# A quantised convolution network: VectorE convolves two of eight tiles, ScalarE writes the normalised rows, the down projection moves one slot later

## What is computed

```python
x = x + _L1_ffn_ref(_layernorm(x), w1, conv_w, conv_b, w2)

def act_quant(x):
    scale = 127.0 / clip(max(abs(x), axis=-1), 1e-05)
    return clip(round(x * scale), -128, 127) / scale
h = bit_linear(x, w1)                       # act_quant(x) @ ternary w1, 256 -> 1024
h = depthwise_conv1d(h, conv_w, conv_b)     # 3 taps along the sequence, one set per channel
h = silu(h)
x_add = bit_linear(h, w2)                   # act_quant(h) @ ternary w2, 1024 -> 256
```

## Time and profile before

| | |
|---|---|
| median of 3 runs | 1712.03 us (1707.19 to 1712.98) |
| the profiled execution | 1712.71 us, span 1710.6 us |
| busy, share of the span | PE 86%, PEld 64%, DVE 61%, ACT 44%, POOL 7% |
| this stage | first up projection at 511.98, last residual ends at 674.14 |
| mean granted TensorE clock | 0.941 of full speed |

### The profile page before, as it was taken

How to read it: one execution, slowest core, us unless ns; L and a number is a source line. 1 busy time by engine, 2 the same in 40 slices (tenths; PEclk the granted TensorE clock), 3 DMA queues, 4 the chain that set the end, 5 groups by cost and what they waited for, 6 DMA issues and landing times.

```text
span 1710.6 us, 27127 instructions
## 1 busy us (share of the span) xinstructions
PE 1475.4 (86%) x9940; PEld 1101.9 (64%) x9947; DVE 1035.3 (61%) x2319; ACT 749.7 (44%) x1249; POOL 111.5 (7%) x153
## 2 busy tenths in 40 slices
PE   6999999878879895799889999999988999997356
PEld 4666665557764443477767878787864777786345
DVE  4455564778868764787746161625248988975434
ACT  2211212267763664676732122222224877885122
POOL 1000000000000000111000000000001101000323
PEclk9999999999989997999989999999998999998579
DMA  9451101400000000000029600000100000000176
GB/s 323 160 172 61 61 14 48 165 13 13 13 2 1 0 1 12 12 13 13 2 104 341 187 1 2 1 2 2 32 7 6 2 7 7 2 2 1 48 256 224
DMA packets 59540, 99.82 MB, mean 58 GB/s; under 512 B 10739, under 2 KB 48748, under 8 KB 59246
## 3 DMA queue, kind: packets, MB, share of 16 engines
q1 hardware_dynamic: 57022, 82.57, 14.8%
q10 hardware_dynamic: 512, 11.11, 1.9%
q0 software_dynamic: 1872, 4.27, 0.7%
HBM read 76.23 MB, written 38.35 MB: 67 GB/s over the span
## 4 chain that ended last, share of the span: by engine, by line
PE 49%; issue 23%; DVE 12%; ACT 5%; DVEq 4%; DMA 3%; POOL 1%; SPq 1%; ACTq 1%; POOLq 1%
PE bank L1906 7%; PE bank L1907 7%; PE bank L1611 6%; PE bank L1628 5%; PE bank L1965 3%; PE bank L1712 3%; PE bank L1763 2%; DVE MB L844 2%; DVE plo L862 2%; DMA jx<-copy_routed 2%; PE bank L1683 1%; PE bank L1645 1%; PE bank L1717 1%; PE bank L1716 1%; DVEq L1120 1%
## 5 line engine op out<-in xcount | busy, mean ns | idle before, releaser
L862 DVE TENSOR_TENSOR plo<-e,phi 120x512 f16<-120x512 f32 x256 | 179.9, 708 | 46.6 <-ACT phi L1363 43.3
L1357 ACT ACTIVATE e<-bank 120x512 f32<-120x512 f32 x256 | 150.6, 588 | 39.3 <-PE bank L1717 32.1
L1363 ACT ACTIVATE phi<-e 120x512 f16<-120x512 f32 x256 | 161.5, 631 | 8.8
L844 DVE TENSOR_REDUCE MB<-bank 128x4 bf16<-128x480 f32 x256 | 156.2, 649 | 14.4 <-PE bank L1685 10.5
L1611 PE MATMUL bank<-xT,winT 128*127 128x512 f32 (+1 forms) x256 | 114.8, 594 | 4.7 <-ACTq L1276 4.7
L1628 PE MATMUL bank<-woutT,msk 128*128 128x256 f32 (+1 forms) x512 | 115.2, 379 | 0.0
L1305 ACT ACTIVATE act<-bank,bin 127x512 f32<-127x512 f32 x64 | 43.6, 687 | 151.6 <-DVE dec L732 145.1
L1628 PEld LDWEIGHTS bank<-woutT,msk 128*128 128x128 f32 (+1 forms) x512 | 97.0, 190 | 16.3 <-DVE msk L724 0.3
L1906 PE MATMUL bank<-hah,h1w 128*128 128x512 f32 x256 | 101.3, 396 | 3.3 <-DVE hal L654 3.3
L548 POOL TENSOR_TENSOR veps<-mv,ceps 128x4 f32<-128x4 f32 x32 | 6.4, 201 | 1483.6 <-DVEq L622 1346.9
L1712 PE MATMUL bank<-Q_even,Kpad_even 128*120 128x256 f16 x512 | 100.6, 279 | 2.0 <-ACT e L1357 2.0
(11 more groups left out here) (305 smaller groups left out, 3606.3 us busy)
## 6 DMA issues: line engine op xcount, KB each, us to landing
copy_routed<-zeros SPq DMA_DIRECT2D x1, 17028.0 KB
jw<-copy_experts SPq DMA_DIRECT2D x23, 641.0 KB
seen<-in_h1T SPq DMA_DIRECT2D x8, 512.0 KB, 5.6
seen<-in_h2T SPq DMA_DIRECT2D x8, 512.0 KB, 6.3
h1w<-copy_h1T SPq DMA_DIRECT2D x1, 4096.0 KB, 17.0
h2w<-copy_h2T SPq DMA_DIRECT2D x1, 4096.0 KB, 14.1
ctxp<-in_ctxT SPq DMA_DIRECT2D x13, 240.0 KB, 2.8
jx<-copy_routed SPq DMA_DIRECT2D x23, 132.0 KB
```

Source lines behind the costliest of these rows:

```text
L844: dve.tensor_reduce(MB[:, t, h0 // 8, SK + h0 % 8:SK + h0 % 8 + 4], b[:, 0:4 * SK].rearrange("p (h k) -> p h k", h=4), AX.X, ALU.max).then ...
L862: dve.tensor_tensor(plo[:, g % 3, :], e32[:, g % 3, :], phi[:, g % 3, :], ALU.subtract).then_inc(s.lo, 1)
L1357: act.activation(e32[:, g % 3, :], bank[2 + g % 3][0:SK, :], ACT.Exp).then_inc(s.exp, 1)
L1363: act.activation(phi[:, g % 3, :], e32[:, g % 3, :], ACT.Copy).then_inc(s.phi, 1)
```

## The change

VectorE convolves tiles 0 and 4 of each pair itself (`conv_tile`): a tensor_scalar for the first tap and two scalar_tensor_tensor for the others, written straight into hc; TensorE leaves these tiles out, and the tap matrices for them are not built. `convolved(g)` picks the semaphore of the engine that convolved a tile. silu of such a tile reads and writes hc. `next_rows` goes from VectorE to ScalarE (slot 1), with `shift` for the fourth stage on GpSimd, and `quantise_rows` waits for it. `down` moves from slot 0 to slot 1 on TensorE, `down_residual` from slot 1 to slot 2 on VectorE.

```diff
--- before.py
+++ after.py
@@ -35,6 +35,7 @@
 CELL = D + 8
 JOBS = NT + NE - 1
 NB, NO = 6, 4
+VTILES = (0, 4)
 SEEN = (2 * K2 + 2 * HT) // PAIRS
 W1, W2, B1, B2, KIT = 0, K2 * D, 2 * K2 * D, 2 * K2 * D + K2, 2 * K2 * D + K2 + D
 
@@ -349,8 +350,8 @@
     Ff.xs, Ff.m0, Ff.g1, Ff.low, Ff.lowsum, Ff.long = (
         sem("f_" + n) for n in ("xs", "m0", "g1", "low", "lowsum", "long"))
     Df = Signals()
-    Df.xq, Df.xqt, Df.xqT, Df.sb, Df.sB, Df.up, Df.deq, Df.conv = (
-        sem("d_" + n) for n in ("xq", "xqt", "xqT", "sb", "sB", "up", "deq", "conv"))
+    Df.xq, Df.xqt, Df.xqT, Df.sb, Df.sB, Df.up, Df.deq, Df.conv, Df.vconv = (
+        sem("d_" + n) for n in ("xq", "xqt", "xqT", "sb", "sB", "up", "deq", "conv", "vconv"))
     Df.silu, Df.mag, Df.maxed, Df.mt, Df.dgh, Df.qb, Df.hm, Df.hq, Df.out = (
         sem("d_" + n) for n in ("silu", "mag", "maxed", "mt", "dgh", "qb", "hm", "hq", "out"))
     Hf = Signals()
@@ -374,6 +375,10 @@
             s.oT, s.oTs, s.out, s.half, s.bo = (sem(L.name + "_" + n) for n in ("oT", "oTs", "out", "half", "bo"))
         X[L.name] = s
     X["l3x"] = X["l2x"]
+
+    def convolved(g):
+        n = sum(q % HT in VTILES for q in range(g + 1))
+        return (Df.vconv, n) if g % HT in VTILES else (Df.conv, g + 1 - n)
 
     def next_pair(i):
         return (i + 1) % PAIRS
@@ -568,7 +573,7 @@
                                        ALU.add).then_inc(X["l2x"].bo, 1)
                 if p == 2:
                     pool.wait_ge(xln_ready, 4 * p + i + 1)
-                rstd_of(i + (4 * p + 2), p in (2, 4, 6))
+                rstd_of(i + (4 * p + 2), p in (2, 3, 4, 6))
 
         pool.iota(acc[:, 0, :], pattern=[[PLACES // 128, NE]], base=0, channel_multiplier=0,
                   allow_small_or_imprecise_dtypes=True)
@@ -982,6 +987,7 @@
             def quantise_rows(i):
 
                 dve.drain()
+                dve.wait_ge(xln_ready, 4 * 3 + 1 + i)
                 dve.tensor_reduce(amax[:], xln[:], AX.X, ALU.max, apply_absolute_value=True)
                 dve.drain()
                 quantiser(0)
@@ -1006,7 +1012,7 @@
                     dve.wait_ge(Df.sB, i + 1)
                 dve.wait_ge(Df.up, g + 1)
                 if g >= 3:
-                    dve.wait_ge(Df.conv, g - 2)
+                    dve.wait_ge(*convolved(g - 3))
                 dve.tensor_tensor(hpad[:, g % 3, :, 1:S + 1], bank[g % 2][:, :].rearrange("p (b s) -> p b s", b=2),
                                   sB[:, i % 2, :].rearrange("p (b s) -> p b s", b=2), ALU.mult).then_inc(Df.deq, 1)
 
@@ -1017,6 +1023,16 @@
                     before = mags[:, (g - 1) % 2, :] if t == 1 else mrun[:, i % 2, :]
                     last = dve.tensor_tensor(mrun[:, i % 2, :], mags[:, g % 2, :], before, ALU.max)
                     last.then_inc(Df.maxed, 1 if t > 1 else 2)
+
+            def conv_tile(g):
+                t, y = g % HT, hc[:, g // HT % 2, g % HT, :].rearrange("p (b s) -> p b s", b=2)
+                dve.drain()
+                dve.tensor_scalar(y, hpad[:, g % 3, :, 0:S], cw[:, t, 0:1], None, ALU.mult)
+                for j in (1, 2):
+                    dve.drain()
+                    last = dve.scalar_tensor_tensor(out=y, in0=hpad[:, g % 3, :, j:j + S], scalar=cw[:, t, j:j + 1],
+                                                    in1=y, op0=ALU.mult, op1=ALU.add)
+                last.then_inc(Df.vconv, 1)
 
             def quantise_hidden(i):
                 dve.wait_ge(Df.mt, i + 1)
@@ -1052,13 +1068,6 @@
                 for t in range(TT):
                     dve.bn_aggr(mv[:, t, :], stats[:, t, :])
                 dve.drain().then_inc(ln_var, 1)
-
-            def next_rows(i):
-                dve.wait_ge(ln_rstd, i + (4 * 3 + 2))
-                for t in range(TT):
-                    dve.tensor_scalar(xln[:, t, :], x[:, TT * next_pair(i) + t, :],
-                                      mv[:, t, 0:1], rstd[:, t:t + 1], ALU.subtract, ALU.mult)
-                dve.drain().then_inc(xln_ready, 1)
 
             dve.memset(magic[:, 0:1], MAGIC)
             dve.memset(magic[:, 1:2], -MAGIC)
@@ -1071,16 +1080,16 @@
                 i, t = g // HT, g % HT
                 dve.drain()
                 if g < TILES3:
-                    if i == 0:
+                    if i == 0 and t not in VTILES:
                         tap_weights(t)
                     dequantise(g)
+                if g < TILES3 and t in VTILES:
+                    conv_tile(g)
                 if 2 <= g < TILES3 + 2:
                     largest(g - 2)
                 if t == 0 and i < PAIRS:
                     next_stats(i)
-                if t == 1 and i < PAIRS:
-                    next_rows(i)
-                if t == 1 and i >= 2:
+                if t == 2 and i >= 2:
                     down_residual(i - 2)
                 if t == 2 and i < PAIRS - 1:
                     quantise_rows(i + 1)
@@ -1417,10 +1426,11 @@
 
             def silu(g):
                 i, t = g // HT, g % HT
-                act.wait_ge(Df.conv, g + 1)
+                act.wait_ge(*convolved(g))
                 if i >= 2 and t == 0:
                     act.wait_ge(Df.hm, HT * (i - 1))
-                act.activation(hc[:, i % 2, t, :], bank[2 + g % 2][:, :], ACT.Silu,
+                y = hc[:, i % 2, t, :] if t in VTILES else bank[2 + g % 2][:, :]
+                act.activation(hc[:, i % 2, t, :], y, ACT.Silu,
                                bias=cb[:, t:t + 1]).then_inc(Df.silu, 1)
 
             def magnitude(g):
@@ -1429,6 +1439,14 @@
                     act.wait_ge(Df.maxed, g - 1)
                 act.wait_ge(Df.silu, g + 1)
                 act.activation(mags[:, g % 2, :], hc[:, i % 2, t, :], ACT.Abs).then_inc(Df.mag, 1)
+
+            def next_rows(i):
+                act.wait_ge(Df.xq, i + 1)
+                act.wait_ge(ln_rstd, i + (4 * 3 + 2))
+                for t in range(TT):
+                    last = act.activation(xln[:, t, :], x[:, TT * next_pair(i) + t, :], ACT.Identity,
+                                          bias=nmr[:, t:t + 1], scale=rstd[:, t:t + 1])
+                last.then_inc(xln_ready, 1)
 
             def rounded(g):
                 i, t = g // HT, g % HT
@@ -1446,6 +1464,8 @@
                 if 1 <= g <= TILES3:
                     silu(g - 1)
                     magnitude(g - 1)
+                if t == 1 and i < PAIRS:
+                    next_rows(i)
                 if t == 3 and i < PAIRS - 1:
                     dequant_scales(i + 1)
                 if t == 4 and i < PAIRS - 1:
@@ -1872,9 +1892,9 @@
                 i, t = g // HT, g % HT
                 if g < TILES3:
                     up(g)
-                if 1 <= g <= TILES3:
+                if 1 <= g <= TILES3 and (g - 1) % HT not in VTILES:
                     conv(g - 1)
-                if t == 0 and i >= 2:
+                if t == 1 and i >= 2:
                     down(i - 2)
                 if g == TILES3:
                     pe.wait_ge(xln_ready, 4 * 3 + 5)
```

## The result

The changed kernel takes 1719.98 us (median of 7 runs, 1717.63 to 1726.89) beside 1709.92 for the kernel before in the same session (7 runs, 1705.86 to 1713.53). The ratio is 1.0059, 95% interval 1.0043 to 1.0076: slower by 10 us. The forecast was 1718, slower, range 1710 to 1725. The profiled execution of the changed kernel is its fastest run, 1717.63, and lies only 4.9 over the profiled one of before (1712.71). So the two traces can show some 5 of the 10 us.

What follows compares the result with a forecast made beforehand. The prediction saw a 37 us circle in which ScalarE, TensorE and VectorE are last in turn, VectorE from 578.43 to 594.24. It summed 6.45 - 0.65 - 0.9 + 0.5 = +5.4 on 1712.71 to 1718, range 1710 to 1725.

Steps and rivals of the forecast that it cites:

- Steps 0 and 1: Tile slots 0 to 15: VectorE's added convolutions and the row handover delay tile 7 by 1.6, step 1's first hr by 6.45.
- handover: Rows written by ScalarE after GpSimd's nmean and nmr: statistics to quantise later by about 0.3 in step 0, 0.85 in step 1.
- The price of one VectorE convolution: One tensor_scalar, two scalar_tensor_tensor and three drains on hpad: about 2.1 us, low end 1.8, high end 2.5.
- Step 2: Tile slots 16 to 23: quantise rows 2.75 earlier through the later down, convolution 20 gives back 2.1: -0.65.
- Step 3 and the tail: Slots 24 to 31: one TensorE convolution gone, -3.0, convolution 28 on VectorE +2.1, so -0.9; the tail behind it 0.
- 0 to +1.0 for each of two downs; I take +0.5 together: Down projections on the path: more TensorE pauses lower its clock and lengthen them, +0.5 in the sum.
- The clock rival: Pauses slow TensorE's downs and convolutions (tiles 9, 25) more than taken: +4.1 on the sum, 1722; chance 0.18.
- Nothing changed outside 511 to 680: A sign of being right: the profile shows no change outside the stage's stretch of 511 to 680 us.
- TensorE busy 20 us less: A sign of being right: TensorE's busy time falls by 20 us and its waits rise by as much.
- a dear VectorE convolution: Rival: 2.5 us or above per convolution on tiles 0, 8, 12, 20, 28, partly 4: +2 to +3, 1721; chance 0.12.
- TensorE as the bound: Rival: VectorE's new work falls into its waits in steps 0 and 1 too: -15, 1698; chance 0.07, milder form 0.02.
- the halves cancel: Rival: handover at its low end, convolutions at 1.8, tile 5 less late: +2 to +4, 1715; chance 0.25.

Runs made afterwards that it cites:

- no_vector_conv: The changed kernel with no tile convolved on VectorE; rows on ScalarE and later down projection kept: ratio 0.9978 to the kernel before.
- vector_conv_only: The kernel before with tiles 0 and 4 convolved on VectorE and empty matmuls in TensorE's place, rows and down unmoved: ratio 1.0041.
- vector_conv_hidden: The kernel before with only tiles 16 and 24 convolved on VectorE and empty matmuls in TensorE's place: ratio 1.0011.
- down_later: The kernel before with only the down projection moved to slot 1 and its residual to slot 2: 1701.30 us, ratio 0.9931; repeated, 0.9953.
- before_more: The kernel before with 24 unread two-column matmuls added on TensorE right behind the stage: 1729.59 us, ratio 1.0119.
- after_again: The changed kernel measured once more, nothing altered: 1721.72 us, ratio 1.0046 to the kernel before.

## Why the prediction was right, and where it was not

The direction and the time came as forecast (1718 against 1719.98, slower), but by luck: in the sum two errors cancelled. The forecast change is +5.4 and the measured one +10.1. The two times lie closer than that because the sum started from the profiled 1712.71, 2.8 above the later median of the kernel before.

**Steps 0 and 1: right in mechanism, 0.8 high.** The first hr of step 1 is 5.69 late (45.26 to 50.95), forecast 6.45. The pieces, by start in the stage: hpad 8 1.24 late (forecast 1.6), statistics 3.13, so convolution 8 with its saved wait 1.89 (1.9), handover 0.31 (0.85), and from quantise rows to hr 2.25 (2.1). The piece that missed most is the handover: from GpSimd's start to ScalarE's it took 548.12 - 546.11 = 2.01, where I had 2.46 from an attention stage. The difference is nmean, 0.23 here and 0.65 there, the low end that the prediction names. The price of one VectorE convolution, 2.1, is 2.14. The Trainium skill (SBUF — State Buffer, "Who interferes with whom") would let nmr come later beside a running maximum. In this trace nothing of that shows: the maximum ran from 546.84 to 547.52, wholly beside GpSimd's rstd (546.64 to 547.68), and took the 0.68 that it takes elsewhere, rstd its 1.04, and nmr began 0.14 behind it.

**Step 2: right.** -0.85, of which 0.17 is the down (4.36 for 4.53), so -0.68 for the rest against -0.65. Both halves of that are shown: without the convolutions, on no_vector_conv, step 2 is 4.59 shorter, about 1.6 of it by the faster down, and on vector_conv_only the convolution costs 2.1. Its quantise rows had no wait for ScalarE's rows, as forecast.

**Step 3 and the tail: right apart from the clock, which was wrong in sign.** Step 3 gave -2.60 and the tail up to its first hr -1.68. Take from each the 1.67 of its down (2.90 for 4.57): -0.93 (forecast -0.9) and -0.01 (forecast 0). This takes the down to count one for one. The prediction has the -3.0 because a convolution is gone from between the down and amax, and the runs say by which edit: taking tile 24 off TensorE alone brought 0.4 (vector_conv_hidden), the later down alone 3.0 without its clock (down_later). The bracket of 0.96 in the earlier trace rows already said that VectorE stood close behind TensorE there. "0 to +1.0 for each of two downs; I take +0.5 together" was the step that failed. I read 4.53 as a nearly full-rate down with a short dip, and priced only the way down to 5.52. But 2.90 is the full rate, 4.4 to 4.6 are already half slow, and there was more to win than to lose. The four downs gave -3.75 in all instead of +0.5. I held that the change gives TensorE more pauses ahead of the downs, but it moved pauses to other places (19.8 us of waits for hpad) and made TensorE late for two of the three downs. By the counts above that helps the clock but does not settle it: before_more won 1.67 on one down with nothing changed in the stage. How much of the 3.75 belongs to the change is open.

**The clock rival** (pauses lower the clock more than taken) saw slow convolutions: tile 9 took 5.49 as it said, and tiles 21 and 29, each behind TensorE's wait for a VectorE convolution, 4.24 and 5.40 against 2.74; tile 25, which it named, ran at full clock behind a fast down. So one of the prediction's own signs of being wrong, the clock at 0.50 while TensorE convolves, did come. The rival's price did not: VectorE was late enough to cover them, except 0.90 ahead of one hpad in step 3. The Trainium skill (TensorE: Matmul & The Clock Gate, "What's actually happening") says that the low clock is the default and activity releases it; the trace agrees both ways, 0.50 behind the pause ahead of 546.98, and 1.00 at 615.40.

**"Nothing changed outside 511 to 680" is false, and this is the step that the sum lacks.** The stage's own sum is 5.69 - 0.68 - 0.93 - 0.01 - 3.75 = +0.32, as measured. The other 4.7 of the profiled span (7.1 in after_again) lie behind it, with 5.9 and 6.8 lost in the sixth layer. I had counted the removed matmuls as time, and not as instructions whose absence moves all of TensorE's later code.

**"TensorE busy 20 us less"**: 15.2 on the page, since the slow convolutions took back a third. The rivals of a dear VectorE convolution and of TensorE as the bound fall: VectorE shows no wait for TensorE between 540.52 and 563.19, and one convolution costs what the rows of the other stages said. That the halves cancel came near inside the stage (+0.32), by another way.

**What stays open.** The medians differ by 10.1, the two profiled runs by 4.9, so about half of the difference isn't in a trace. The stretch behind the sixth layer took 509.5 to 517.9 in the traces of this study, in no order that the kernels explain, and that of before is among the longest; what sets it wasn't looked into, and no total here can be read from one trace to better than some 4 us. The clock of the downs varies between executions of the same stage code (162.16 and 159.99 for the kernel before; 162.48, 162.49, and 163.41 with the empty matmuls, for the one after), so some of the 3.75 may be missing in other executions. By these traces the stage is +0.3 to +3.4. The gain by the empty matmuls (1.0005 for 1.0046) says how much the placement holds: 7 us of the ratio, 9 against the first measurement.

## What to carry to other kernels

Read a late consumer's wait before moving work off an engine: here TensorE stood in front of a wait for hq, and letting it do the next tile first made the stage 8.65 us shorter, part of it by a down projection without a pause at full clock, while taking two tiles off it brought a slower walk on VectorE. When a change removes or adds instructions on an engine with loops or jumps later on, compare the waits without a releaser behind the changed stage too, and test by adding empty instructions: a result of half a per cent can be nothing but this. Before counting time freed on one engine, ask how long the next one waits for it (0.96 here, where 3.0 were freed and 0.4 gained). Of a group whose duration you take from a row, ask at which clock it ran and what it is at the other.

## What the runs showed of the hardware

- **Waits by the place of the code.** TensorE's loop of the sixth layer took 91.80 a lap before, 92.83 with 24 matmuls fewer ahead of it, 91.61 with 24 empty ones put back, 95.65 with 24 more than before: one to four us more a lap for the same instructions. The added waits come at one place of a lap, behind a jump. Why they come there is an inference.
- **The same down projection ran at two clocks.** 25 matmuls of 128x256 in bf16 took 2.90 at granted clock 1.00, 4.36 to 4.57 with part of it low, and 4.41 to 5.52 in the tail. With no wait for hq ahead of it, all 32 took 3.65 to 3.70 in ten of ten. With a wait, both durations came, also behind equal waits (2.14 and 1.12: 4.57 and 2.90).
- **Empty matmuls aren't free.** The 24 of two columns in fp32 (48 records) took 7.35, 306 ns each, at a mean granted clock of 0.72 (671.2 to 678.5 of before_more).
- **GpSimd's chain for four values** per row took 2.01 from its start to ScalarE's in step 1 and 2.46 in the attention stage; 0.42 of the difference is one operation (nmean, 0.23 and 0.65).
